# Cross-attention and a 64-expert network on one core: squares of K moved from GpSimd to ScalarE, and the order of small steps on five engines changed

## What is computed

```python
x = x + xattn(layernorm(x), ctx)          # 16 heads of 32; q and k get a LayerNorm per head
x = x + ffn(layernorm(x))

# xattn: q = ln(x @ Wq + bq); k, v from the first 496 context rows, k_dca, v_dca from the last 16
ctx = attn(q, k, v) + attn(q, k_dca, v_dca)
return ctx @ Wo + bo

# ffn: 64 experts, each token to its 6 best, capacity 384 rows an expert; and a shared SwiGLU of width 704
scores = softmax(x @ gate_w.T); topk_w, topk_idx = top_k(scores, 6)
eo = (silu(buf @ w_gate) * (buf @ w_up)) @ w_down      # per expert, width 352
return scatter_add(eo * weight) + shared_swiglu(x)
```

## Time and profile before

| | us |
|---|---|
| three runs | 1756.02, 1766.42, 1767.89 (median 1766.42) |
| the profiled execution, its own time | 1762.85 |
| span that its trace covers | 1761.1 |
| PE busy | 1693.0 (96% of the span) |
| DVE busy | 1090.3 (62%) |
| ACT busy | 1028.3 (58%) |
| POOL busy | 757.9 (43%) |

### The profile page before, as it was taken

The page is one execution under the profiler, slowest core; times in us unless marked ns, Lnnn a source line. Parts: engine busy times, 40 slices in busy tenths (PEclk is TensorE's granted clock), DMA queues, the critical chain, the costliest instruction groups (busy, mean ns, idle before and its releaser), DMA issues. The chain is left out here.

```text
span 1761.1 us, 35834 instructions
## 1 busy us (share of the span) xinstructions
PE 1693.0 (96%) x11782; PEld 1539.8 (87%) x11782; DVE 1090.3 (62%) x2157; ACT 1028.3 (58%) x1871; POOL 757.9 (43%) x719
## 2 busy tenths in 40 slices
PE   4899999999999999999999999999999999999995
PEld 3588888888888888989999999999999999999984
DVE  7555656777566665443666666666666666666664
ACT  4567766666545553222566666666666666666664
POOL 7513222334223230242245555555555555455554
PEclk8899999999899999999999999999999999999997
DMA  5543433433222532312577777777777777777766
GB/s 189 160 117 91 119 105 97 121 95 98 83 84 79 177 107 87 122 38 86 181 227 232 209 214 226 218 210 223 223 216 205 228 221 213 222 232 206 215 198 212
DMA packets 149083, 289.87 MB, mean 165 GB/s; under 512 B 29199, under 2 KB 66319, under 8 KB 139649
## 3 DMA queue, kind: packets, MB, share of 16 engines
q1 hardware_dynamic: 116112, 238.21, 41.9%
q0 software_dynamic: 32880, 50.51, 13.7%
HBM read 243.73 MB, written 64.52 MB: 175 GB/s over the span
## 5 line engine op out<-in xcount | busy, mean ns | idle before, releaser
L2188 POOL DMA_INDIRECT out<-y,ids_s x128 | 209.9, 1640 | 280.3 <-ACT y L2323 254.8
L2448 PE MATMUL ps<-xt_hi,gu_hi 128*128 128x256 f32 (+1 forms) x1856 | 303.5, 285 | 0.6 <-issue 0.6
L2448 PE MATMUL ps<-xt_lo,gu_hi 128*128 128x256 f32 (+1 forms) x1856 | 289.8, 278 | 0.0
L2448 PE MATMUL ps<-xt_hi,gu_lo 128*128 128x256 f32 (+1 forms) x1856 | 289.2, 278 | 0.0
L2223 DVE TENSOR_TENSOR gu_lo<-raw_gu,gu_hi 128x1408 fp32r<-128x1408 f32 (+2 forms) x132 | 214.6, 1625 | 112.5 <-ACT gu_hi L2220 109.3
L1121 ACT ACTIVATE prob<-ps 128x512 f32<-128x512 f32 x256 | 152.2, 597 | 191.4 <-PE ps L1428 169.6
L2448 PEld LDWEIGHTS ps<-xt_hi,gu_hi 128*128 128x128 f32 (+1 forms) x1856 | 250.6, 181 | 9.0 <-issue 3.0
L2448 PEld LDWEIGHTS ps<-xt_lo,gu_hi 128*128 128x128 f32 (+1 forms) x1856 | 244.4, 181 | 0.0
L2448 PEld LDWEIGHTS ps<-xt_hi,gu_lo 128*128 128x128 f32 (+1 forms) x1856 | 244.2, 181 | 0.0
L2168 POOL DMA_INDIRECT xg<-h_rows,ids_g x128 | 191.6, 1497 | 115.2 <-POOL ids_g L2163 50.6
L2280 ACT ACTIVATE h_hi<-h 128x256 fp32r<-128x256 f32 (+1 forms) x240 | 100.6, 419 | 224.0 <-DVE h L2349 223.4
(11 more groups left out here) (316 smaller groups left out, 3000.3 us busy)
## 6 DMA issues: line engine op xcount, KB each, us to landing
raw_gu<-in_w_gu SPq DMA_DIRECT2D x71, 1408.0 KB, 6.7
raw_d<-in_w_d SPq DMA_DIRECT2D x71, 512.0 KB
raw_d<-in_w_d SPq DMA_DIRECT2D x71, 192.0 KB
qs<-qk_rows SPq DMA_DIRECT2D x192, 64.0 KB, 2.2
ks<-qk_rows SPq DMA_DIRECT2D x192, 64.0 KB, 2.0
xa<-in_x SPq DMA_DIRECT2D x16, 256.0 KB, 3.0
qk_rows<-k_hi SPq DMA_DIRECT2D x16, 256.0 KB, 2.2
qk_rows<-k_lo SPq DMA_DIRECT2D x16, 256.0 KB, 2.5
```

The lines of the kernel that those rows point to most:

```text
L2188: pool.indirect_dma_start(out=out, out_offset=bass.IndirectOffsetOnAxis(B.ids_s[:, p, k:k + 1], 0), in_=B.y[:, p, k, :], in_offset=None, b ...
L2448: last = pe.matmul(gu_banks(it, c)[half], gu_columns(w, it, half, d, c), x[:, x_p, d, 0:W], start=i == 0, stop=i == len(steps) - 1)
```

## The change

1. **Squares of K in the front** go from POOL (L591) to ACT, where the function already exists for attention; in steps 1 to 3 ahead of Q's full part, in steps 4 and 5 behind it.
2. **Row statistics** on DVE in the front are made one step ahead, between `taken` of Q and `taken` of K; `ctx_rest` and `scales` go ahead of Q's low part.
3. **The joined bias** (L555 to L558) goes to the end of POOL's step 3; the numbering of POOL's signals follows.
4. **Routing on DVE**: `route_mask` goes ahead of `weighted(n)`, `route_code` ahead of `weighted(n + 1)`, and the last `maxima` of the unit ahead of `route_slots`.
5. **K's transposition** on PE goes behind `third_key(n + 2)` where no tile u+6 is left (unit 10 alone).
6. **The last head**: all four parts of its weighting go ahead of the output product.
7. **Scatter** in the network: the copy of the indices goes ahead of the wait for the scatter before.
8. **Tail**: the gather runs four blocks ahead instead of three, the fourth already in the last item; the column copies are made a block earlier; SP loads gate/up weights ahead of the down weights of the block before; ACT rounds the first block's down weights ahead of the last item's results.

```diff
@@ POOL, front @@
-                if s == 3:
-                    pool.wait_ge(centred, CENTRED["bd"])
-                    pool.tensor_tensor(bd[:, D:2 * D], bd[:, D:2 * D], bv[:], ALU.add)
-                    without_means(bd[:, 0:D].rearrange("p (g d) -> p g d", d=HD), sums_bd[:], H)
...
+            def bias_of_dca(s):
+                if s == 3:
+                    pool.wait_ge(centred, CENTRED["bd"])
+                    pool.tensor_tensor(bd[:, D:2 * D], bd[:, D:2 * D], bv[:], ALU.add)
+                    without_means(bd[:, 0:D].rearrange("p (g d) -> p g d", d=HD), sums_bd[:], H)
...
             def front(s):
-                squares(s - 2, kb, sq_k, k_bias, k_sum, k_sq, True)
                 weights_first(s)
                 scaled(s - 2, kb, H, k_sum, kn_ready)
                 scaled(s - 2, qb, 0, q_sum, qn_ready)
                 weights_then(s)
-                squares(s - 1, qb, sq_q, q_bias, q_sum, q_sq, False)
+                squares(s - 1, qb, sq_q, q_bias, q_sum, q_sq)
                 k_rest(s - 2)
+                bias_of_dca(s)
@@ DVE, front @@
                 if s > 1:
-                    row_stats(s)
                     summed(s - 2, sq_q, 0, q_sq, q_sum)
                     summed(s - 2, sq_k, H, k_sq, k_sum)
+                    ctx_rest(s - 1)
+                    scales(s - 7)
                     if s < 6:
                         rest(s - 3, q_full, q_hi, q_lo, q_high, q_low, q_out)
-                    ctx_rest(s - 1)
-                    scales(s - 7)
                     front_dca(s)
                 j = s - 1
                 taken(j, P, qb, front_q(j), bq, q_ready, trq_ready, q_raw, q_bias)
+                if s < 6:
+                    row_stats(s + 1)
                 taken(j, keys_of(j), kb, front_k(j), bk, k_ready, trk_ready, k_raw, k_bias)
@@ DVE, attention @@
                 route_top(u - 6)
+                route_mask(u - 6)
                 weighted(n)
-                route_mask(u - 6)
...
                 take_pos(u - 6)
+                route_code(u - 6)
                 weighted(n + 1)
-                route_code(u - 6)
...
                 rest(u + 5, k_full, k_hi, k_lo, k_high, k_low, k_out)
+                maxima(n + 4, 1)
                 route_slots(u - 6)
-                maxima(n + 4, 1)
@@ ACT, front @@
                 if s == 1:
                     xt_high(1, FX)
+                    squares(0, kb, sq_k, k_bias, k_sum, k_sq, True)
...
+                if s < 4:
+                    squares(s - 1, kb, sq_k, k_bias, k_sum, k_sq, True)
                 turned_full(s - 2, FQ_T, trq_ready, q_full, 0, False, q_low)
+                if 4 <= s < 6:
+                    squares(s - 1, kb, sq_k, k_bias, k_sum, k_sq, True)
@@ PE, attention @@
-                k_turned(u + 5)
+                if tile(u + 6):
+                    k_turned(u + 5)
                 third_key(n + 2)
+                if not tile(u + 6):
+                    k_turned(u + 5)
...
             item = net.item
+            weigh(HEADS - 1, 0)
+            weigh(HEADS - 1, 1)
+            weigh(HEADS - 1, 2)
+            weigh(HEADS - 1, 3)
             pe.wait_ge(at_lo.sem, at_lo.value(WAIT1, 1))
             pe.wait_ge(h2T_in.sem, h2T_in.value(WAIT1 - 1, 1))
             wo_half(WAIT1, 0)
-            weigh(HEADS - 1, 0)
-            weigh(HEADS - 1, 1)
             wo_half(WAIT1, 1)
-            weigh(HEADS - 1, 2)
-            weigh(HEADS - 1, 3)
@@ POOL, network: scatter @@
         p = it.half
+        pool.tensor_copy(B.ids_s[:, p, 0:nb], slots_of(it, B.ids)).then_inc(s_copied.sem, 1)
         if it.known and it.e == SH_ITEMS:
...
             pool.wait_ge(added.sem, added.value(it.expert - 1, 16 * nb))
-        pool.tensor_copy(B.ids_s[:, p, 0:nb], slots_of(it, B.ids)).then_inc(s_copied.sem, 1)
@@ lead-over to the tail @@
             thirds["gather_first"](pool, 2)
+            thirds["columns"](pool, FIRST)
             scatter(pool, it)
+            thirds["gather_first"](pool, 3)
             thirds["y_freed"](pool)
...
             thirds["act_x"](act, FIRST + 1)
+            thirds["act_d"](act, FIRST)
             results(it)
-            thirds["act_d"](act, FIRST)
@@ SP and POOL, tail @@
         def body(b):
-            e = expert(sp, b + 3)
-            load(e, b + 3, (gu_lo.sem, gu_lo.value(b.j + 1, 2)), (d_lo.sem, d_lo.value(b.j + 1, 1)))
+            load_gu(b + 3, gu_lo, b.j + 1)
+            load_d(b + 2, d_lo, b.j)
...
         def body(b):
-            e = expert(pool, b)
-            pool.tensor_copy(B.wsl3[:, b.p:b.p + 1], B.w[:, bass.ds(e * CB + 2, 1)]).then_inc(w_copied.sem, 1)
-            pool.tensor_copy(B.ids3s[:, b.p:b.p + 1], B.ids[:, bass.ds(e * CB + 2, 1)]).then_inc(s_copied.sem, 1)
-            pool.wait_ge(xt_ready.sem, xt_ready.value(b.j + 1, 1))
-            gather(pool, b + 3)
+            pool.wait_ge(xt_ready.sem, xt_ready.value(b.j + 2, 1))
+            gather(pool, b + 4)
...
                 compute_op=ALU.add).then_inc(added.sem, 16)
+            columns(pool, b + 1)
```

More of the change, by code:

```diff
@@ L209, in attention_phase @@
         SPLIT = dict(wq0=1, wq1=2, cols=3, wk=4, cd=5, kvd0=6, kvd1=7)
-        POOL_SPLIT = dict(bias=1, wv=2, wd_v=3, wd_k_centred=4, bd=5, wd_k=6, wo=6 + DC)
+        POOL_SPLIT = dict(bias=1, wv=2, wd_v=3, wd_k_centred=4, wd_k=5, bd=6, wo=6 + DC)
         def rowvec(v):
@@ L572, in weights_then, with squares @@
                     rest(wd_lo[:, :, 0:D], halves(wd_in_place, 0), wd_hi[:, :, 0:D])
-            def squares(j, v, sq, given, summed, done, dca):
+            def bias_of_dca(s):
[3 more added lines that the diff above has]
+                    without_means(bd[:, 0:D].rearrange("p (g d) -> p g d", d=HD), sums_bd[:], H)
+            def squares(j, v, sq, given, summed, done):
                 if not tile(j):
@@ L577, in squares @@
                 pool.wait_ge(given.sem, given.value(j, 1))
-                if dca and j % T == T - 1:
-                    pool.wait_ge(kd_in.sem, kd_in.value(j // T, 16))
                 if j >= 1:
@@ L2608, in sync, with load_gu, load_d @@
     def sync(sp):
-        def load(e, b, gu_done, d_done):
-            src = ins["w_d"][bass.ds(e, 1)].rearrange("a f n -> (a f) n")
-            sp.wait_ge(*gu_done)
+        def load_gu(b, done, turn):
+            e = expert(sp, b)
+            sp.wait_ge(done.sem, done.value(turn, 2))
             sp.dma_start(B.raw_gu[:, b.p].rearrange("p a n -> p (a n)"),
                          ins["w_gu"][bass.ds(e, 1)].rearrange("a p n -> p (a n)")).then_inc(gu_in[b.p].sem, 16)
-            sp.wait_ge(*d_done)
+        def load_d(b, done, turn):
+            e = expert(sp, b)
+            src = ins["w_d"][bass.ds(e, 1)].rearrange("a f n -> (a f) n")
+            sp.wait_ge(done.sem, done.value(turn, 1))
             sp.dma_start(B.raw_d[:, b.p, 0:2, :], src[0:2 * P, :].rearrange("(c p) n -> p c n", p=P)).then_inc(d_in[b.p].sem, 16)
@@ L2619, in sync @@
         for k in range(2):
-            load(expert(sp, FIRST + k), FIRST + k, (S.gu_lo.sem, S.gu_lo.value(LAST_ITEM.weights - 1 + k, 2)),
-                 (S.d_lo.sem, S.d_lo.value(LAST_ITEM.weights - 1 + k, 1)))
-        load(expert(sp, FIRST + 2), FIRST + 2, (gu_lo.sem, gu_lo.value(0, 2)), (d_lo.sem, d_lo.value(0, 1)))
+            load_gu(FIRST + k, S.gu_lo, LAST_ITEM.weights - 1 + k)
+            load_d(FIRST + k, S.d_lo, LAST_ITEM.weights - 1 + k)
+        load_gu(FIRST + 2, gu_lo, 0)
         def body(b):
-            e = expert(sp, b + 3)
-            load(e, b + 3, (gu_lo.sem, gu_lo.value(b.j + 1, 2)), (d_lo.sem, d_lo.value(b.j + 1, 1)))
+            load_gu(b + 3, gu_lo, b.j + 1)
+            load_d(b + 2, d_lo, b.j)
         each(sp, body)
@@ L2637, in gather, with columns @@
             bounds_check=N - 1, oob_is_err=False).then_inc(rows_in[b.p].sem, 16)
+    def columns(pool, b):
+        e = expert(pool, b)
+        pool.tensor_copy(B.wsl3[:, b.p:b.p + 1], B.w[:, bass.ds(e * CB + 2, 1)]).then_inc(w_copied.sem, 1)
+        pool.tensor_copy(B.ids3s[:, b.p:b.p + 1], B.ids[:, bass.ds(e * CB + 2, 1)]).then_inc(s_copied.sem, 1)
     def gather_first(pool, k):
@@ L2645, in gather_first @@
         else:
-            pool.wait_ge(xt_ready.sem, xt_ready.value(0, 1))
+            pool.wait_ge(xt_ready.sem, xt_ready.value(k - 2, 1))
         gather(pool, FIRST + k)
@@ L2673, in body @@
                 compute_op=ALU.add).then_inc(added.sem, 16)
+            columns(pool, b + 1)
         many = each(pool, body)
         for p in range(2):
-            pool.wait_ge(rows_in[p].sem, (many + (4 - p)) // 2 * 16)
+            pool.wait_ge(rows_in[p].sem, (many + (5 - p)) // 2 * 16)
         pool.wait_ge(S.added.sem, S.added.value(LAST_ITEM.expert, 16 * nb))
@@ L2720, in scalar @@
         for p in range(2):
-            loads = (many + (4 - p)) // 2
-            act.wait_ge(gu_in[p].sem, loads * 16)
-            act.wait_ge(d_in[p].sem, loads * 32)
+            act.wait_ge(gu_in[p].sem, (many + (4 - p)) // 2 * 16)
```

(3 more changed lines are left out.)

## The result

The changed kernel takes 1805.62 us (median of 4 runs, 1800.63 to 1809.84) against 1765.72 (4 runs of the kernel before): 1.0243 times as long, 95% interval 1.0212 to 1.0275. The forecast was 1758, in a range of 1743 to 1774. The profiled execution has a span of 1807.6 us against 1761.1.

A forecast was written before the change was run, and what follows sets the result against it. PE was taken as the bound, nearly always busy, so only waits or slow-clock stretches could shrink. Terms summed to -7.85 us from the profiled 1762.85, giving 1755.0, and 1758 with 3.6 to the median; range 1743 to 1774.

The forecast's parts named there:

- rival A: Attention, units 12 to 15: longer waits for weighted each bring a clock fall of 5.6 us, giving 1780; chance 0.10.
- the +7.1: Attention, units 11 to 15: mask and code ahead of the weightings delay PE, 1.42 us a unit (0 to +12.9).
- the near end: Mask and code cost 0: PE returns sums later, so DVE idles longer and does the code there for nothing.
- 5.6 a time: Units 12 to 15: price of each new clock fall, taken from unit 10's slow stretch; four give 22.4 us.
- Unit 10's slow stretch, -5.6: Attention, 440 to 460 us: PE's wait for K brought the clock down; removing it gains 5.6 us (-5.6 to 0).
- rival C: Unit 10's slow stretch stays, not caused by the wait for K, or comes elsewhere: 1764; chance 0.16.
- The front, -1.6: Front: squares on ACT and reordered statistics shorten the chain to K's scaling, gaining 1.6 us (-5.3 to +0.7).
- Maxima ahead of route_slots, -2.6: Attention: four PE idles at the transposed maxima, 0.84 and three of 0.60, all go: -2.6 us (-2.6 to 0).
- K's transposition, -0.15: Attention, unit 10: PE's 0.85 wait for POOL's scaling goes, but later work has waits: -0.15 us (-0.85 to 0).
- Last head, -1.3: End of attention: four weighting parts fill PE's 1.27 wait for h2T, gaining 1.3 us (-1.3 to 0).
- Scatter and tail, -3.7: Tail: scatter starts 1.9 us earlier and issues 2.9 faster, full gain 4.8; -3.7 taken (-4.8 to +1.8).
- Rival D: Front: the square needs another ACT table, two loads in each of five steps cost 12.8 us, giving 1771; chance 0.06.

The follow-up runs named there:

- e3: The kernel before with one edit, route_mask ahead of weighted(n): 1809.7 us, ratio 1.0275.
- e2: The changed kernel with route_mask and route_code both put back behind the weightings, all other edits kept: 1754.25 us, ratio 0.9970 against the kernel before.
- e5: The kernel before with route_mask ahead of weighted(n), and six throw-away products on PE ahead of the waiting weighting in units 12 to 15: 1775.91 us, ratio 1.0064.
- e6: The kernel before with route_mask ahead of weighted(n) in unit 13 alone: 1772.85 us, ratio 1.0058.
- e4: The kernel before with the front's edits alone (squares of K, row statistics and scales, joined bias): 1763.51 us, ratio 1.0019.
- e10: e7 with route_top moved behind weighted(n) as well, ahead of route_mask: 1806.34 us, ratio 1.0211 against the kernel before.
- e1: The changed kernel with route_mask alone put back behind weighted(n), route_code still moved: 1771.48 us, ratio 1.0040 against the kernel before.
- e7: The kernel before with only last maxima ahead of route_slots, K's transposition in unit 10, scatter and tail edits: 1758.91 us, ratio 0.9965.
- e11: e7 with the squares of K on ACT and the joined bias last: 1754.63 us, ratio 0.9961 against the kernel before.
- e12: e11 with one short throw-away product on PE ahead of the waiting weighting in units 12 to 15: 1756.52 us, ratio 0.9973 against the kernel before.

## Why the prediction was wrong

The direction was wrong, by rival A, which I priced too low and held too unlikely (0.10). By its steps:

- **"With the mask in front, `weighted(n)` and with it PE's next weighting come 1.42 later"**, and the +7.1 made from it, is the step that failed. It prices the longer wait as a delay and nothing else, and puts what the wait does to the clock at nothing. The mask alone (e3) costs 46.9 us, and in the changed kernel putting mask and code back (e2) takes 51 off the median. With the same delay and the wait filled (e5) 11 are left, and one wait alone (e6) costs 8.1.
- **As a delay** the term was close. In units 12 to 15 the mask costs 1.36 each, and the code beside it nothing, which was the near end and its mechanism (PE returns its sums later). In e5, with the clock kept up, units 12 to 14 together are 3.1 us longer than in the kernel before. Unit 12 waited 0.49 already and not 0.23, so its wait became 1.85. In units 6 to 9, put at nothing, both moves cost 1.6 (145.36 against e2's 143.78).
- **"If each brings a stretch like that one, 5.6 a time"**: rival A had the right mechanism, in the right units, 12 to 15, and too small a size. 5.6 was right for the fall that it was read from (unit 10 takes 38.48 with it and 32.82 in e4, with the same wait and without it), which held the lower clock for 13.6 us. The four new ones held it for 20.5 to 30.7 us and cost, beyond the 1.36 of their waits, 7.3, 10.2, 10.2 and 13.5 (the last reaches over the last head and the output products): 41.2 together, or 1758 + 41.2 = 1799. In all of these, and in e6, a microsecond at the lower clock costs about 0.4 us (0.36 to 0.44). So it was the length of a fall that was mis-sized.
- **"Against: PE waits 1.27 at 612.73, and no fall stands there."** One counterexample carried the low chance. Counting over all traces shows why it should not: waits of 1.58 to 1.85 for `weighted(n)` brought a slow stretch 9 times of 9 (changed kernel 4, e3 4, e6 1); waits of 1.00 in e10 6 of 6; K's wait of 0.84 to 1.06 in unit 10 4 of 7; the waits of 0.66 to 1.20 behind the code's move (changed kernel and e1) 4 of 7; the wait of 0.46 to 0.50 in unit 12 2 of 10 (e7, e11); and the 1.27 of rows 7 one (e6, low from 626.4 to 629.8) of the eight in which the clock stood at the upper level before it. What follows a wait depends on its length and its place; a rule for it I can't give.
- **Unit 10's slow stretch, -5.6, and rival C.** With K's wait gone the unit takes 32.4 instead of 38.5 in e2 and e7, so -6.1: right in size. "I take it that this wait brought it about" was too strong: with the wait untouched it came 4 times of 7. In the changed kernel itself another one stands behind the code's wait of 0.66, 456.12 to 459.96 (10.2 us by the granted clock); the same wait in unit 11, 0.68, had none behind it.
- **The front, -1.6.** Wrong in sign: +1.6 at the first head by the means (85.9 against 84.3). The squares gained more than I gave them (3.6). I priced the row statistics by their 0.68 and did not ask what they wait for. Moved a step ahead, they wait for a DMA that SP may issue only when ACT has used the x tile of two steps before, 2.8 to 4.3 us, with `taken` of K and xT's low part behind them.
- **Maxima ahead of route_slots, -2.6.** Right way, 1.6: after the first unit only about 0.21 of each 0.6 came through.
- **K's transposition, -0.15.** 0.4 without counting the clock.
- **Last head, -1.3.** In the one trace that can tell, +0.5: from head 63's maxima to the network's first product 30.89 in e2 against 30.41 and 30.44 in e4 and e7. But e2's low clock from 608.2 to 611.6 lies in it: the last six parts take 1.24 instead of 0.81, and the first twelve products 4.17 instead of the 3.02 of the twelve at 616.51. Less these 1.6 it would be -1.1, an estimate near the forecast. New waits came all the same: the four parts in a row wait for ACT's exponentials, and the output product, all behind them, no longer covers what comes next. PE in e2:

```profile
605.04 0.44 PE L1450 MATMUL ps<-v_last,prob 128*128 128x66 f32 x2 [0.69 <-ACT prob L1122]
...
607.99 1.24 PE L1453 MATMUL ps<-v_main,prob 128*128 128x33 f32 x6
609.04 4.17 PE L1470 MATMUL ps<-wo,aT 128*128 128x512 f32 x12
...
616.51 3.02 PE L1470 MATMUL ps<-wo,aT 128*128 128x512 f32 x12 [1.99 <-DVE aT L709]
```

- **Scatter and tail, -3.7.** Right. From the network's first product to the end the old order takes 1122.1 to 1125.5 (seven traces, mean 1124.4), the new one 1118.0 to 1121.3 (seven, 1119.8): 4.6 shorter. The copy off the path and the issue of 1.59 in place of 4.75 are both seen, though the scatter starts only 1.2 and not 1.9 us earlier, and the second issue is 1.0 longer.
- **Rival D** did not come: `sq_k` on ACT takes 0.63 in the front (72.25, above) and no table load stands there. The page "ScalarE: Activation LUTs" of the Trainium skill (Table sets) does not name the square among the functions of every set; here it needed no load, neither beside the square root (front) nor beside the exponentials (attention).

Without the clock, the terms as measured (front +1.6, maxima -1.6, mask 5.4, mask and code in units 6 to 9 +1.6, transposition -0.4, last head -1.1, tail -4.6) come to about +1; what decided is that one slow stretch was shortened and four were added. What was not found is why a wait of under 1.3 us is followed by a fall in one execution and not in another.

## To carry to other kernels

Before a step goes ahead of one that TensorE already waits for, price the wait twice: as a delay, and as standing still, which here cost five to ten times the delay through the clock. Where such a wait cannot be avoided, a product into a free bank may be cheaper than silence: it was for waits of 1.6 (e5), and made no difference that can be told for waits of 0.2 to 0.5 (e12). And for a step moved ahead, ask what it waits for, not only how long it runs: a queue in order passes a DMA's latency on to all that stand behind it.

## What was not expected of the hardware

- Throw-away products made a kernel faster: e5 against e3, 1775.91 against 1809.7, each beside its own runs of the kernel before (1764.75 and 1762.84).
- The low clock, once there, stayed though PE had no wait any more: in the changed kernel 20.00 of 20 busy at 0.50 from 560 to 580, in e6 27.3 us in all, from 541.1 on, with no wait behind 541.44.
- A short wait does not decide it alone. The same stretch of the kernel with the same 0.84 to 0.85 us went both ways (unit 10 in e4 and in e6), and e7 and e11 had a fall in unit 12 behind a wait of 0.49; eight other traces have this wait too (0.46 to 0.50) and no fall. What decides there was not found.
- The front of identical instruction orders ends anywhere from 82.87 to 85.51, with PE at either clock in parts of it. An edit worth 2 us there can't be judged by the time of the whole kernel.
